# Set-up, layer-norm row and quarter waits of a recurrent layer: eighteen squarings, another order of preparations, conv and M's chain

## What is computed

```python
xn = layernorm(x)                                   # no affine part
x_norm = layernorm(xn) * ln_g + ln_b
x_norm = x_norm + conv3(x_norm) + conv_b            # depthwise, along time
gate, input_gate = split(x_norm @ gate_w.T + gate_b)
Bm = x_norm * sigmoid(input_gate) @ B_w.T + B_b     # 64 states
Cm = x_norm @ C_w.T + C_b
A_bar = expm(dt_A * A)                              # 64 x 64, once
s = layernorm(s @ A_bar + Bm[t]) * st_g + st_b      # 2048 steps, one after another
y = Cm[t] * s
attn = (y @ D_w.T + D_b) * sigmoid(gate)
ffn = xn @ W.T + b + (xn @ V_r) @ C.T
out = x + attn * silu(ffn)
```

## Time and profile before

| | |
|---|---|
| median of 3 runs | 2530.65 us (2530.29 to 2530.93) |
| the profiled execution | 2531.44 us, span 2529.6 us |
| PE busy | 2478.2 us, 98% |
| DVE busy | 2200.3 us, 87% |
| POOL busy | 1271.0 us, 50% |
| ACT busy | 1009.8 us, 40% |
| granted clock of PE, mean | 0.994 of full speed |
| first step on DVE | 81.41 us after the span's start |

### The profile page before, as it was taken

The page is one execution under the profiler, slowest core; times in us unless marked ns, Lnnn a source line. Parts: engine busy times, 40 slices in busy tenths (PEclk is TensorE's granted clock), DMA queues, the critical chain, the costliest instruction groups (busy, mean ns, idle before and its releaser), DMA issues.

```text
span 2529.6 us, 42562 instructions
## 1 busy us (share of the span) xinstructions
PE 2478.2 (98%) x10057; PEld 1309.0 (52%) x10057; DVE 2200.3 (87%) x10947; ACT 1009.8 (40%) x1837; POOL 1271.0 (50%) x2465
## 2 busy tenths in 40 slices
PE   8899999999999999999999999999999999999996
PEld 5455555555555555555555555555555555555544
DVE  5788898888899888899888899888899888899887
ACT  3444344444334444334444334444334444334310
POOL 1355555455555455555455555455555455555443
PEclk9999999999999999999999999999999999999997
DMA  3112112122121122121122121221121221121121
GB/s 110 25 42 59 38 43 52 46 59 55 37 49 51 47 59 52 38 50 48 50 59 50 38 52 47 51 59 48 37 55 47 51 59 46 37 57 47 34 58 36
DMA packets 99606, 125.19 MB, mean 49 GB/s; under 512 B 31967, under 2 KB 48543, under 8 KB 99360
## 3 DMA queue, kind: packets, MB, share of 16 engines
q1 hardware_dynamic: 98624, 121.30, 19.5%
q10 hardware_dynamic: 736, 1.18, 0.2%
HBM read 71.96 MB, written 33.55 MB: 42 GB/s over the span
## 4 chain that ended last, share of the span: by engine, by line
POOL 49%; DVE 33%; issue 13%; PE 3%; POOLq 0%; DMA 0%; DVEq 0%; ACT 0%; ACTq 0%; SPq 0%
POOL dw L401 44%; DVE wq L860 14%; DVE dw L871 9%; DVE dw L885 9%; POOL ln L423 5%; PE bank L1116 1%; PE bank L1200 0%; PE bank L1195 0%; PE bank L1217 0%; POOLq L234 0%; POOL ln L425 0%; POOL ln L426 0%; POOL ln L427 0%; PE bank L1054 0%; POOL ln L440 0%
## 5 line engine op out<-in xcount | busy, mean ns | idle before, releaser
L401 POOL TENSOR_TENSOR dw<-q,minus_half 8x1 f32<-8x1 f32 x2048 | 1107.1, 541 | 1170.5 <-DVE wq L860 1140.0
L1180 PEld LDWEIGHTS bank<-Mscan,wT 128*65 128x65 f32 x2046 | 216.4, 136 | 654.5 <-issue 645.1
L1105 PE MATMUL bank<-xnorm,gateT 128*128 128x512 f32 x1024 | 506.4, 593 | 0.0
L860 DVE SCALAR_TENSOR_TENSOR wq<-dw 8x65 f32<-8x65 f32 x2048 | 443.2, 216 | 70.3
L1116 PE MATMUL bank<-xnorm,gateT 128*128 128x512 f32 x1024 | 501.8, 596 | 0.0
L1097 PE MATMUL bank<-xnT,WT 128*128 128x512 f32 x1024 | 494.0, 593 | 0.0
L1180 PE MATMUL bank<-Mscan,wT 128*65 128x128 f32 x2046 | 406.7, 280 | 25.3 <-DVE wT L888 15.3
L1181 PE MATMUL bank<-Mscan,wT 128*65 128x128 f32 x2046 | 391.7, 273 | 0.0
L885 DVE SCALAR_TENSOR_TENSOR dw<-dw 8x64 f32<-8x64 f32 x1024 | 280.0, 273 | 124.2 <-POOL dw L401 92.2
L871 DVE SCALAR_TENSOR_TENSOR dw<-dw 8x64 f32<-8x64 f32 x1024 | 280.6, 274 | 85.9 <-POOL dw L401 80.6
L875 DVE SCALAR_TENSOR_TENSOR dw<-bank,dw 8x128 f32<-8x128 f32 x1024 | 342.1, 334 | 1.9 <-PE bank L1181 1.6
(11 more groups left out here) (158 smaller groups left out, 2775.4 us busy)
## 6 DMA issues: line engine op xcount, KB each, us to landing
xc<-in_x SPq DMA_DIRECT2D x252, 128.0 KB, 2.8
xa<-in_x SPq DMA_DIRECT2D x252, 128.0 KB, 2.7
out<-o SPq DMA_DIRECT2D x248, 128.0 KB, 2.4
dw<-dtok SPq DMA_DIRECT2D x128, 96.0 KB
wtok<-dw SPq DMA_DIRECT2D x128, 33.0 KB
gateT<-in_gateT SPq DMA_DIRECT2D x1, 2048.0 KB
WT<-in_WT SPq DMA_DIRECT2D x1, 1024.0 KB, 8.0
xa<-in_x SPq DMA_DIRECT2D x4, 256.0 KB
```

Of the source, the lines that this page charges most:

```text
L401: nc.gpsimd.tensor_tensor(dw[0:B, t, CR:CR + 1], q[:], minus_half[0:B, 0:1], ALU.pow).then_inc(s["r_ready"], 1)
L860: V.scalar_tensor_tensor(out=wq[:], in0=w_eps, scalar=1.0 / S, in1=w_eps, op0=ALU.mult, op1=ALU.mult, accum_out=q[:]).then_inc(s["q_ready" ...
L1105: ins = mm(mbank["gate", m][:], gateT[:, k, P * m:P * m + P], xnorm[p][:, k, :], start=(k == 0), stop=(k == KH - 1))
L1180: mm(scanP[0:WIDE, 0:2 * S], wT[:, 0:WIDE], Mscan[:, 0, :], start=True, stop=False)
```

## The change

It does six things.

- `SQUARINGS` goes from 20 to 18, with the mask and the tables that have its width, and the work between squarings has other places: z transposes at n = 4 to 7, conv from n = 6, input-gate pieces from n = 8, the statistics all within the squarings, the gated products at n = 16 and 17.
- `keep_busy` and its matmuls are gone. Two of the four low-rank products come ahead of the norm of A and two behind it.
- The seven preparations come at terms 8 to 11 of the series (two, two, two, one), on a semaphore of their own, `vec_ready`. ACT's first normalisation and M's chain on PE wait for all seven.
- M's chain: the transpose comes first, then the bias products; `fill_d` comes ahead of the products for vT, for dw and for Mscan; DVE's copies follow in that order.
- In the steps: POOL's first layer-norm instruction for chunks from 3 on is dropped (the mean is read where ACT put it), 12 instructions at t = 34 to 45 are left, and ACT's row means wait for all 12. The wait for `D_IN` comes ahead of L889 and not behind it.
- In chunk 0, PE's z transposes come at t = 3 and 6 and not 0 and 3, DVE's conv at t = 7 to 22 and not 3 to 10, 11 to 14 and 17 to 20. In the last chunk the gate pieces and two gated halves start earlier.

```diff
-SQUARINGS = 20
+SQUARINGS = 18
-POOL_LN = range(33, 46)
-PE_GATE_LAST = range(25, 41)
-V_G_LAST = (30, 31, 34, 37, 38, 41, 42, 45)
+POOL_LN = range(34, 46)
+PE_Z_FIRST = (3, 3, 6, 6)
+V_CONV_FIRST = range(7, 23)
+PE_GATE_LAST = (21, 24, 25, 26) + tuple(range(29, 41))
+V_G_LAST = (29, 30, 34, 37, 38, 41, 42, 45)
-PE_Z0 = (4, 6, 8, 10)
-DVE_CONV = (8, 10, 12, 14)
-PE_IG0 = (10, 11, 12, 12, 13, 14, 14, 15, 16, 16, 17, 18, 18, 19, 20, 20)
-PE_X0 = (17, 17, 19, 19)
-DVE_XG0 = (18, 19)
-DVE_STATS2 = (17, 18, 19)
+PE_Z0 = (4, 5, 6, 7)
+DVE_CONV = (6, 8, 10, 12)
+PE_IG0 = (8, 9, 9, 10, 10, 11, 12, 12, 13, 14, 14, 15, 15, 16, 16, 17)
+PE_X0 = (13, 13, 15, 15)
+DVE_XG0 = (16, 17)
+DVE_STATS2 = (15, 16, 17, 17)
+DVE_VEC = (8, 9, 10, 11)
...
 # POOL, ln_op(n, k), n >= 3
-                    m0, scale, var = sums[:, 0, :], (1.0, 1.0 / H), sums[:, 1, :]
+                    m0, scale, var = sums[:, 0, :], (None, 1.0 / H), sums[:, 1, :]
+                if n >= 3:
+                    nm = m0
-                ] if n < 3 else first + [
+                ] if n < 3 else first[1:] + [
...
 # ACT
-                wait_ln(act, n - 1, 3)
+                wait_ln(act, n - 1, LN_OPS)
-            act.wait_ge(s["dve_setup"], SETUP_VEC)
+            act.wait_ge(s["vec_ready"], VEC_OPS)
...
 # DVE, odd_step
                 V.transpose(wT[0:32, 0:S], dw[:, t, CD:CM]).then_inc(s["wT_ready"], 1)
-                V.scalar_tensor_tensor(... a_ready ...)
                 if t % QT == QT - 1:
                     of, q = divmod(i * NQ + t // QT + 1, NQ)
                     if of < NC:
                         wait_for(dve, D_IN[q], 16, of, 16)
+                V.scalar_tensor_tensor(... a_ready ...)
...
 # DVE, behind a term of the series
+                for k in range(VEC_OPS):
+                    if DVE_VEC[k // 2] == TERMS - n:
+                        vec_op(k)
...
 # PE
-            for k in range(KH):
-                mm(wbank[k][:], VT[:, P * k:P * k + P], CrT[:], start=True, stop=True).then_inc(s["wprime_mm"], 1)
-            keep_busy(4)
+            for k in range(2):
+                low_rank(k)
             ... norm of A ...
+            for k in range(2, KH):
+                low_rank(k)
             for n in range(TERMS):
                 ...
-                keep_busy(1)
...
+            pe.wait_ge(s["vec_ready"], VEC_OPS)
+            tp(scanP[0:S, S:2 * S], M, ident[0:S, 0:S])
             mm(scanP[0:S, 0:1], AC[:], sm("st_b"), start=True, stop=False)
-            mm(scanP[0:S, 0:1], Bb[:], ones[0:1, 0:1], start=False, stop=True)
-            tp(scanP[0:S, S:2 * S], M, ident[0:S, 0:S])
-            mm(scanP[0:S, 2 * S:2 * S + B], AC[:], st_b_wide[:, 0:B], start=True, stop=True)
-            mm(scanP[0:B, 3 * S:4 * S], st_b_wide[:, 0:B], AC[:], start=True, stop=True).then_inc(s["pe_setup"], 1)
+            mm(scanP[0:S, 0:1], Bb[:], ones[0:1, 0:1], start=False, stop=True).then_inc(s["pe_setup"], 1)
             ... b_proj(0, 0), MT x M, b_proj(0, 1 to 3) ...
+            pe.wait_ge(s["dve_setup"], SETUP_M + 3)
+            for q in range(NQ):
+                fill_d(0, q, -1, False)
             ... the products for vT, dw and Mscan, then the one for p_ready, then c_proj ...
```

More of the change, by code:

```diff
@@ L417, in ln_op @@
                 wait_ln(pool, n, k)
-                if k == 3:
+                if k == (3 if n < 3 else 2):
                     wait_for(pool, "z_done", NJ, n, 0)
@@ L625, in _ @@
             input_gate(0, 3)
[L626 removed]
+            act.wait_ge(s["dve_setup"], SETUP_M + 2)
             copy_dT(0)
@@ L894, in odd_step, with vec_op @@
                         wait_for(dve, D_IN[q], 16, of, 16)
[L897 to L901, removed]
-            gates = slice(vcol["gate_b"], vcol["in_gate_b"] + 1)
-            link(V.tensor_scalar(vec[:, gates, :], vec[:, gates, :], 0.5, None, ALU.mult))
-            link(V.tensor_scalar(sm("C_b"), sm("C_b"), 0.5, None, ALU.mult))
-            assert done[0] == SETUP_VEC
+                V.scalar_tensor_tensor(out=dw[0:B, t, CM:CM2], in0=dw[0:B, before, CM2:SLOT], scalar=r,
+                                       in1=dw[0:B, t, CM:CM2], op0=ALU.mult, op1=ALU.add).then_inc(s["a_ready"], 1)
+            gates = slice(vcol["gate_b"], vcol["in_gate_b"] + 1)
+            row = absrow[0:1, 7:8]
+            vec_ops = [
+                lambda: V.tensor_scalar(vec[:, vcol["conv_w1"], :], vec[:, vcol["conv_w1"], :], 1.0, None, ALU.add),
+                lambda: V.tensor_reduce(row, Bb[:], AX_X, ALU.add),
+                lambda: V.tensor_scalar(vec[:, gates, :], vec[:, gates, :], 0.5, None, ALU.mult),
+                lambda: V.tensor_scalar(row, row, -1.0 / S, None, ALU.mult),
+                lambda: V.tensor_scalar(sm("C_b"), sm("C_b"), 0.5, None, ALU.mult),
+                lambda: V.tensor_scalar(Bb[:], Bb[:], row, None, ALU.add),
+                lambda: V.tensor_scalar(st_b_wide[:], st_b_wide[:], sm("st_b"), None, ALU.mult),
+            ]
+            assert len(vec_ops) == VEC_OPS
+            def vec_op(k):
+                wait_for(dve, "vec_ready", 1, k, 0)
+                vec_ops[k]().then_inc(s["vec_ready"], 1)
             link(V.tensor_scalar(As[:].rearrange("p a b -> p (a b)"), small[:, 0:2 * S], sm("dt"), None, ALU.mult))
@@ L966, in _ @@
                         right_tap(0, DVE_CONV.index(n - 1), h, 0)
-                if n in DVE_STATS2:
-                    bn_stats(2, DVE_STATS2.index(n), 0)
-                    bn_stats(2, DVE_STATS2.index(n), 1)
+                for j in range(NJ):
+                    if DVE_STATS2[j] == n:
+                        for h in range(2):
+                            bn_stats(2, j, h)
+                if n == DVE_STATS2[-1]:
+                    aggregate(2)
                 if n in DVE_XG0:
@@ L1001, in iteration @@
                 gate_at = V_G if A else V_G_LAST
+                conv_at = V_CONV if i else V_CONV_FIRST
                 for t in range(CT):
@@ L1256, in _ @@
             ins.then_inc(s["pe_setup"], 1)
-            for q in range(NQ):
-                fill_d(0, q, -1, False)
+            pe.wait_ge(s["dve_setup"], SETUP_END)
+            mm(scanP[0:B, 0:2 * S], vT[:], Dcat[0:S, S:], start=True, stop=True).then_inc(s["p_ready"], 1)
             pe.wait_ge(s["dve_setup"], SETUP_END)
@@ L1280, in iteration @@
                         for k in range(KH):
-                            if PE_Z[k] == t:
+                            if (PE_Z if i else PE_Z_FIRST)[k] == t:
                                 fill_z(i + 1, k, i, middle)
```

44 lines of the change are left out of this document (17 added, 27 removed).

## The result

| | before | after |
|---|---|---|
| median of 4 runs each | 2530.79 us | 2507.75 us (2506.96 to 2511.74) |
| ratio, 95% interval | | 0.9912, 0.9895 to 0.9929 |
| profiled execution | 2531.44 us | 2511.74 us |
| its span, granted clock | 2529.6 us, 0.994 | 2509.8 us, 0.992 |

The change gains 23.0 us by the medians, not 7.6. The forecast of 2523.0 and its whole range (2518.5 to 2528.0) were too slow; the direction was right. The spans differ by 19.8 us (the profiled execution of after was its slowest), and these are the ones taken apart here; what the three faster executions of after had shorter, 3.4 to 4.8 us, no trace shows.

The account below looks back on a forecast made before the run. The prediction took the recurrence, 2048 steps of one POOL power between two DVE instructions, as the bound. Set-up 3.6, quarter wait 3.5, layer-norm row 0.15 and chunk 0 0.33 sum to 7.6: 2530.65 to 2523.0 us, range 2518.5 to 2528.0.

Parts of the forecast that it names:

- POOL at 0.54: Steps: sign that the chain's power instruction on POOL keeps its time of 0.54 us; no term in the sum.
- Layer-norm row: Steps: dropping POOL's first of 13 layer-norm instructions in 29 chunks gains 0.15 us, or 1.3 if position counts.
- the power instruction settles at another level: Rival, steps: power at 0.552 loses 24 us (2547), at 0.532 gains 16 (2507); chance 0.03 each.
- Quarter wait: Steps t = 31 and 63, and four in chunk 0: moved DMA wait saves 0.055 us at 64 places, 3.5 us.
- The rival that it only moves: Rival, steps: the quarter wait delays the multiply or stays on an inserted instruction, no gain there; 2526.5, chance 0.08.
- Set-up up to M: Set-up's chain of times: first squaring at 23.85 instead of 29.60, M's first PE instruction at 65.75 against 68.85.
- A wait that takes part back: Set-up: ScalarE's first normalisation waits for all seven preparations, PE stalls 2 us; second squaring's gain 3.7, first's 5.75.
- No conv half or piece was late: Rival, set-up squarings: conv or pieces wait at n = 8 and 12, set-up gives nothing; 2526.6, chance 0.07.
- End of set-up: From the last squaring to the first step: PE idle 3.1 us behind DVE's statistics; first step at 77.8 instead of 81.41.
- PE's clock falls in the new idle time: Rival, end of set-up: low clock, first step at 81.9, step 2 up to 5.5 later; say 2530, chance 0.06.
- Chunk 0: Chunk 0: step 2's wait for PE shrinks, transposes moved to t = 3 and 6, gain 0.33; DVE's moved conv costs nothing.
- The last chunk: Last chunk: the earlier gates were forecast to change nothing.

Follow-up runs that it names:

- e1: Kernel before with only the layer-norm row changed: POOL's first of 13 instructions dropped; 2514.63 us, ratio 0.9935.
- e3: Changed kernel with the layer-norm row and the quarter wait put back as before; 2531.57 us, ratio 1.0.
- e2: Kernel before with only the wait for the next quarter's DMA moved ahead of the odd step's last multiply; 2526.37 us, ratio 0.9985.
- f1: Kernel before with the row's one-scalar product left at step 33 and the other twelve instructions one step later, at 35 to 46; 2529.69 us, ratio 0.9999.
- f4: Kernel before with the one-scalar product in chunk 0's row only, times 1.0 plus 0.0 in the 29 later rows; 2529.75 us, ratio 1.0002.
- e8: Changed kernel with seven unread matmuls (three before M's chain, four in chunk 0) and chunk 0's fourth z transpose at t = 8; 2504.54 us, ratio 0.9895.
- e11: e8 with the row's two two-scalar instructions as tensor products and sums with constant tiles, 14 instructions at t = 33 to 46; 2506.17 us, ratio 0.9906.
- e9: Kernel before with the layer-norm row's one-scalar product as its third instruction, behind the two of two scalars; 2530.13 us, ratio 0.9999.
- e10: Kernel before with one of the row's four 128x1 powers made a 128x4 power; 2539.89 us, ratio 1.0044.
- e5: Kernel before with the first of 13 layer-norm instructions written as times 1.0 plus 0.0 (two scalars); 2514.86 us, ratio 0.9937.
- e6: Kernel before with the first of 13 layer-norm instructions a product with a tile of ones; 2514.07 us, ratio 0.9934.
- f6: Kernel before with the whole 13-instruction layer-norm row one step later, t = 34 to 46; 2514.41 us, ratio 0.994.
- e7: Changed kernel with the dropped one-scalar instruction back, but last, at t = 46, its result unread; 2509.09 us, ratio 0.9914.

## Why the forecast was wrong, step by step

**The step that failed** is the forecast's "POOL at 0.54": it kept the power instruction at its slower time, gave that no term in the sum, and priced the dropped instruction (*Layer-norm row*) at 0.15 us. The runs showed the power instruction back at its faster time, 8.7 ns less in each of some 2000 steps, for that instruction alone: 16.0 us in e1, and 0.9935 of the time. The mechanism and its size did stand in the prediction, as the rival "the power instruction settles at another level": 16 us, 2507, chance 0.03. What was wrong is the choice between the two. It was put down as a coin that may fall either way because nothing told why the level changes. But the trace of before said more, in the line of the power instruction up to the first one-scalar product at 121.9 us and from two powers behind it on:

```profile
L401 POOL TENSOR_TENSOR dw<-q,minus_half x34: 529/534/545, 82.0 to 121.4; 8x1 f32<-8x1 f32 x34
L401 POOL TENSOR_TENSOR dw<-q,minus_half x2012: 540/540/553, 125.0 to 2515.0; 8x1 f32<-8x1 f32 x183
```

The level changed at that product's own position, for good, and the product is removed. Without a reason against it the likeliest outcome was that the powers stay as they were ahead of it. The slower side, 0.552, had only the powers right beside the row for it. *Layer-norm row* was sized from the two steps that looked longer, over 29 chunks where the row runs in 30, and missed 0.008 us in each of the others; beside the level it measured 0.5 (the 1.0 of the two steps, less their own 0.0078 each).

That the rival's 2507 lies within 1 us of the 2507.75 is in part luck. It takes the level's 16 and adds the forecast's 7.6; in the profiled execution set-up and chunk 0 gave 1.2 us of their 3.9, and e3 shows no gain from them.

**Quarter wait**: right. 3.5 us forecast, 3.6 by the steps of after, 4.2 by e2's median. The mechanism is in the traces too: the inserted instruction ahead of L871 (L876 in after), which the prediction has the power's wait go to, stays until the power is done at t = 31 of chunk 16 before, and is passed at once in after.

```profile
L222 DVEq EVENT_SEMAPHORE  x1: 294/294/294, 1336.3 to 1336.3; - x1
L225 DVEq EVENT_SEMAPHORE  x1: 21/21/21, 1325.2 to 1325.2; - x1
```

The rival that it only moves is dead: no other step grew.

**Set-up up to M**: right, within 0.9 us at each mark. Forecast and after, in us:

| | forecast | after |
|---|---|---|
| transpose of the row sums | 7.0 | 7.14 |
| series, first on PE | 11.6 | 11.79 |
| series, DVE's first and last | 12.1, 22.9 | 12.30, 22.76 |
| first squaring | 23.85 | 23.65 |
| squaring n = 8 | 39.2 | 39.03 |
| clock at its upper level | 44.2 | 43.3 |
| last squaring | 61.2 | 60.71 |
| reduction that starts M's chain | 64.75 | 64.06 |
| M's first instruction on PE | 65.75 | 65.06 |

*A wait that takes part back* is there too, ACT's normalisation and PE's stall behind it, for the earlier trace rows:

```profile
23.38 2.93 ACT L483 ACTIVATE o<-xc,ln 128x512 f32<-128x512 f32 x4 [14.72 <-DVE st_b_wide L911]
...
26.36 1.11 PE L1206 MATMUL bank<-ident,o 128*128 128x128 f32 x4 [2.02 <-ACT o L483]
```

No conv half or piece was late.

**End of set-up**: the idle time was right (3.1 us, measured 2.85) and what followed from it had 0.06, as the rival "PE's clock falls in the new idle time". It happened. Its price was too high by about half: the first DVE step came at 79.59, not 81.9, and the second half of the loss fell not on step 2 but on step 26 of chunk 0 (2.25 us for 1.18). The idle gap of 2.62 us without a fall was taken as evidence for a margin. It was one execution: all twelve profiled kernels with the old set-up have that gap, of 2.60 to 2.62 us, nine show a fall behind it, near 82 to 85 us, and only before, f1 and f4 don't. That is also why e3 gained nothing: the 1.2 us of its earlier first step went in chunk 0. The Trainium skill (TensorE: Matmul & The Clock Gate, Part 1) has idling return the clock to half rate. The runs agree, in four of four executions behind the gap of 2.85 us and in nine of twelve behind that of 2.6, so this rival deserved far more than 0.06.

**Chunk 0**: the wait in step 2 is gone, as forecast (1.17 us against 1.51). "Nothing" for what was moved was wrong. Of after, chunk 0, PE and DVE around step 8:

```profile
87.65 1.04 PE L1070 MATMUL bank<-ident,z 128*128 128x128 f32 x8
88.52 1.02 PE L1113 MATMUL bank<-xnT,WT 128*128 128x512 f32 x2
89.39 0.38 PE L1196 MATMUL bank<-Mscan,wT 128*65 128x128 f32 x2
89.60 0.38 PE L1197 MATMUL bank<-Mscan,wT 128*65 128x128 f32 x2
```

```profile
90.02 0.34 DVE L880 SCALAR_TENSOR_TENSOR dw<-bank,dw 8x128 f32<-8x128 f32 x1 [0.47 <-PE bank L1197]
```

Both z groups of t = 6 and the feed-forward matmuls stand before this look-ahead, and DVE waits 0.47 for it. Moved earlier, work doesn't vanish from PE, it is in front of the next product. In e8, with one group at t = 8, step 8 takes 1.21 and step 10 takes 1.42.

**The last chunk**: 0.17 us lost, nothing forecast. Its last stretch at the low clock begins at 2487.2, 8.1 us ahead of the last power, against 3.5 before (2511.5 and 2515.0), and steps 58, 60 and 62 take 1.58, 1.43 and 1.55 us where of these only 62 was long (1.47); the level's 0.5 us covers most of it.

## What to carry to other kernels

Plot the duration of every instance of the instruction that the critical chain repeats, to the nanosecond and by position: a change of 8 ns that begins at a named instruction is multiplied by all that follow, and if the change under study touches that instruction, staying at the earlier level is the first hypothesis, not a rival of three in a hundred. The cheapest experiment is the same row one step earlier or later. And an idle time that the clock survived in one execution shows no margin: compare several. Once the cycle is faster, expect PE to take the next gain, as it took four fifths of e11's.

## What the runs showed of the hardware that was not expected

- One TENSOR_SCALAR with a single scalar on POOL (128x4) put all later TENSOR_TENSOR powers from 527 to 534 ns up to 538 to 540, once and until the end of the program (f4: 2012 of them), in e9 and e10 as well with other neighbours. With two scalars, or as a tensor product of the same values, it did nothing (e5, e6). At an even step, t = 34 in f6 and 46 in e7, each one lengthened the power behind it by 12 to 22 ns (546 to 547 and 552 to 555) and no more.
- Set-up's three rows have the one-scalar form too (by -1.0, with no power of the chain ahead of it), and up to its own row chunk 0 was at the faster level in every kernel.
- At the faster level, outside the row's steps, powers alternate by 5 ns from step to step; at the slower one they differ by less than 1.
- A 128x4 power took 1.01 to 1.05 us, a 128x1 and an 8x1 power 0.53 to 0.54 alike: here three more columns cost 0.5 us and 120 more partitions nothing.
- PE's clock fell in nine of twelve profiled executions at a point where the profile of before showed none, and each fall in chunk 0 cost 1 to 2 us there.
